# Two transformer blocks on one core: the first attention's causal mask moved from TensorE to VectorE, its subtraction to GpSimd, and a new order

## The reference

```python
def _mha(x, kv, Wq, Wk, Wv, mask, causal):          # 16 heads of 8
    energy = einsum('bhsk,bhtk->bhst', Q, K)
    lengths = sum(energy[:, :, 0, :] != 0, axis=-1)
    energy = where(cols >= lengths, -inf, energy)
    if causal:
        energy = where(cols[None, :] > cols[:, None], -inf, energy)
    score = softmax(energy / sqrt(dk))
    return einsum('bhst,bhtk->bhsk', score, V) * m

z  = _mha(x, x, Wq1, Wk1, Wv1, mask0, causal=True);         x1 = _layernorm(x + z)
z  = _mha(x1, context, Wq2, Wk2, Wv2, mask1, causal=False); x2 = _layernorm(x1 + z)
z  = (relu(x2 @ fc1_w.T + fc1_b) * mask0) @ fc2_w.T ...;    x3 = _layernorm(x2 + z)
scores = q_heads @ k_heads + bias + bias                    # second block, 16 heads of 64
out = _layernorm(softmax(scores) @ v_heads @ wo + bo + x3)
```

## Time and profile before

| | us |
|---|---|
| median of 3 runs | 342.96 |
| lowest, highest | 342.07, 342.99 |
| the profiled execution | 342.57 |
| its span, from the first to the last instruction | 340.8 |
| busy: TensorE, VectorE, GpSimd, ScalarE | 329.0, 290.3, 242.1, 240.8 |

### The profile page before, as it was taken

One profiled execution on the slowest core, in us unless ns is written; L12 is line 12 of the kernel. 1 busy time (PEld: TensorE's weight loads), 2 busy tenths in 40 slices (PEclk: granted clock), 3 DMA queues, 4 the chain that ended last, 5 costly groups with the idle time before them and its releaser, 6 DMA issues.

```text
span 340.8 us, 13283 instructions
## 1 busy us (share of the span) xinstructions
PE 329.0 (97%) x5363; PEld 255.6 (75%) x5363; DVE 290.3 (85%) x836; ACT 240.8 (71%) x567; POOL 242.1 (71%) x376
## 2 busy tenths in 40 slices
...
GB/s 153 339 305 223 2 2 2 2 4 4 125 2 64 3 12 2 63 80 56 11 4 72 10 63 4 80 4 2 2 2 136 4 70 2 3 20 125 17 2 25
DMA packets 13180, 17.88 MB, mean 52 GB/s; under 512 B 1600, under 2 KB 10176, under 8 KB 13120
## 3 DMA queue, kind: packets, MB, share of 16 engines
...
HBM read 15.99 MB, written 1.05 MB: 50 GB/s over the span
## 4 chain that ended last, share of the span: by engine, by line
PE 72%; DVE 12%; ACT 6%; issue 3%; POOL 3%; DMA 1%; SPq 1%; DVEq 0%; POOLq 0%
PE C_E L630 6%; PE C_E L575 6%; PE A_E L429 4%; PE C_E L620 4%; PE A_E L448 4%; PE C_E L591 4%; PE B_E L429 3%; PE B_E L448 3%; PE C_E L607 3%; PE B_E L346 3%; PE B_E L462 2%; PE A_E L462 2%; PE B_E L545 2%; PE B_E L547 2%; PE B_E L546 2%
## 5 line engine op out<-in xcount | busy, mean ns | idle before, releaser
L1019 POOL TENSOR_TENSOR A_kblk<-A_qk,cst 128x1024 f32<-128x1024 f32 x16 | 30.4, 1899 | 27.1 <-DVE A_qk L863 26.9
L1040 POOL TENSOR_TENSOR L_xg<-L_xh,vec_sb 128x128 f32<-128x128 f32 x64 | 30.2, 471 | 15.3 <-DVE L_xh L937 15.2
L1029 POOL TENSOR_TENSOR L_rstd<-L_ve,cst 128x1 f32<-128x1 f32 x64 | 35.2, 550 | 5.0
L1071 POOL TENSOR_TENSOR Sc<-Sc,C_mx 128x512 f32<-128x512 f32 x28 | 29.2, 1044 | 9.7 <-DVE C_mx L977 9.5
L761 ACT ACTIVATE qT<-C_E,bq 128x128 f32<-128x128 f32 x112 | 31.3, 380 | 4.0 <-PE C_E L575 3.8
L1027 POOL TENSOR_TENSOR L_ve<-L_mv,cst 128x1 f32<-128x1 f32 x64 | 12.3, 193 | 28.7 <-DVE L_mv L928 28.3
L1019 POOL TENSOR_TENSOR B_kblk<-B_qk,cst 128x1024 f32<-128x1024 f32 x16 | 30.4, 1899 | 0.5 <-DVE B_qk L863 0.3
L1080 POOL TENSOR_TENSOR Pc<-Pc,C_rd 128x512 f32<-128x512 f32 x28 | 29.0, 1044 | 1.2 <-DVE C_rd L987 1.0
L575 PE MATMUL C_E<-x3T,wq_sb 128*128 128x128 f32 x224 | 29.0, 277 | 0.4 <-ACT x3T L753 0.4
L575 PEld LDWEIGHTS C_E<-x3T,wq_sb 128*128 128x128 f32 x224 | 27.1, 192 | 1.1 <-ACT x3T L753 0.5
L630 PE MATMUL C_E<-wo_sb,C_zT 128*128 128x128 f32 x224 | 27.6, 276 | 0.1
...
## 6 DMA issues: line engine op xcount, KB each, us to landing
...
```

What stands on the lines that cost most here:

```text
L1019: tt(a.kblk[:], a.qk[:, 1].unsqueeze(1).to_broadcast([P, 8, P]), at["rmask"].unsqueeze(2).to_broadcast([P, 8, P]), ALU.mult).then_inc(a.s_ ...
L1029: tt(l.rstd[:], l.ve[:], at["power"], ALU.pow).then_inc(l.s_rstd, 1)
L1040: tt(l.xg[:], l.xh[:], l.g, ALU.mult).then_inc(l.s_xg, 1)
L1071: tt(v, v, place(n).mx[:, 8 * g:8 * g + 8].unsqueeze(2).to_broadcast([P, 8, S]), ALU.subtract).then_inc(C.s_sub, 1)
```

## The change

Chain A's mask leaves TensorE. The four products with eye64 and later are gone, and later becomes a tile of single-precision numbers. VectorE now adds it as it copies the energies out of PSUM (masked), and takes the maximum from the copy in SBUF (masked_max). The subtraction of the maximum is done in place by GpSimd (a_sub). Chain B keeps its way.

Beside this: the transpose of x3 goes to the second of C's banks, waits less, and leaves part of its waits to the projection behind it; the scaling of the last norm is a scalar_tensor_tensor with the reciprocal deviation as a broadcast tensor; of the 16 groups of fillers at the end 6 are left; and PLAN is another list.

```diff
+COOL = 6
-        eye64, later = sb("eye64", [P, S], BF16), sb("later", [P, S], BF16)
+        later = sb("later", [P, S])
...
             def warm_last(n):
+                if n >= COOL:
+                    return
                 pe.wait_ge(L2.s_xh, PAIRS)
                 idle_products(Bc.X[:, :], 3)
...
                             last = mm(bank[S * b:S * b + S, :], a.qk[r, 0, S * b:S * b + S],
-                                      a.kblk[r, :, S * b:S * b + S], start=True, stop=not causal,
-                                      skip_group_check=True)
-                    if causal:
-                        for hf, bank in enumerate((a.E, a.X)):
-                            r = slice(S * hf, S * hf + S)
-                            for b in range(2):
-                                last = mm(bank[S * b:S * b + S, :], eye64[r, :],
-                                          later[r, :].unsqueeze(1).to_broadcast([S, 8, S]),
-                                          start=False, stop=True, skip_group_check=True)
+                                      a.kblk[r, :, S * b:S * b + S], start=True, stop=True)
                     last.then_inc(a.s_e, 1)
...
                 elif n <= SPLIT:
                     pe.wait_ge(C.s_s, 2 * n)
-                    if n > 1:
-                        pe.wait_ge(L4.s_y, n - 1)
                 elif n == SPLIT + 1:
                     pe.wait_ge(L1.s_xh, PAIRS)
                 else:
-                    pe.wait_ge(L4.s_y, n - 1)
-                if n == 0:
-                    pe.wait_ge(bvo_ready, 2)
-                tr(place(n).E[0][:, 0:P], h2[n % RING][:], ident).then_inc(C.s_x3t, 1)
+                    pe.wait_ge(C.s_zts, 2 * n - 2)
+                tr(place(n).E[1][:, 0:P], h2[n % RING][:], ident).then_inc(C.s_x3t, 1)
...
                     if n == 0:
                         pe.wait_ge(w_queries, 16)
+                        pe.wait_ge(bvo_ready, 2)
+                    elif g == 0 and n > 1 and n != SPLIT + 1:
+                        pe.wait_ge(L4.s_y, n - 1)
...
-                act.copy(place(n).x3T[:], place(n).E[0][:, 0:P]).then_inc(C.s_x3ts, 1)
+                act.copy(place(n).x3T[:], place(n).E[1][:, 0:P]).then_inc(C.s_x3ts, 1)
...
+            def masked(hf):
+
+                def step(n):
+                    dve.wait_ge(A.s_e, n + 1)
+                    if n:
+                        dve.wait_ge(A.s_pt, 2 * n - 1 + hf)
+                    if hf == 0 and n == 0:
+                        dve.wait_ge(ready, 2)
+                    tt(heads(A.S[:, hf * HALF:(hf + 1) * HALF]), heads((A.E, A.X)[hf][:, :]),
+                       later[:].unsqueeze(1).to_broadcast([P, 8, S]), ALU.add).then_inc(A.s_msk, 1)
+                return step
+
+            def masked_max(hf):
+
+                def step(n):
+                    dve.wait_ge(A.s_msk, 2 * n + 1 + hf)
+                    dve.tensor_reduce(A.mx[:, 8 * hf:8 * hf + 8], heads(A.S[:, hf * HALF:(hf + 1) * HALF]), AX.X, ALU.max
+                                      ).then_inc(A.s_max, 1)
+                return step
...
-                    ts(l.xh[:], l.y, l.mv[:, 0:1], l.rstd[:, 0:1], ALU.subtract, ALU.mult).then_inc(l.s_xh, 1)
+                    if l is L4:
+                        dve.scalar_tensor_tensor(l.xh[:], l.y, l.mv[:, 0:1], l.rstd[:].to_broadcast([P, D]),
+                                                 ALU.subtract, ALU.mult).then_inc(l.s_xh, 1)
+                    else:
+                        ts(l.xh[:], l.y, l.mv[:, 0:1], l.rstd[:, 0:1], ALU.subtract, ALU.mult).then_inc(l.s_xh, 1)
...
+            def a_sub(hf):
+
+                def step(n):
+                    pool.wait_ge(A.s_max, 2 * n + 1 + hf)
+                    v = heads(A.S[:, hf * HALF:(hf + 1) * HALF])
+                    tt(v, v, A.mx[:, 8 * hf:8 * hf + 8].unsqueeze(2).to_broadcast([P, 8, S]),
+                       ALU.subtract).then_inc(A.s_sub, 1)
+                return step
...
 PLAN = """
-A.qkv#0 A.qk#0 A.q0#0 A.e0#0 A.nz#0 A.cnt#0 K.warm#0 C.chi#0 A.cut#0 C.whi#0 A.v#0 K.warm#1 A.kblk#0 C.wlo#0
+K.warm#0 A.qkv#0 A.qk#0 A.q0#0 A.e0#0 A.nz#0 C.chi#0 A.cnt#0 K.warm#1 A.cut#0 C.whi#0 A.v#0 K.warm#2 A.kblk#0
...
```

More of the change, by code:

```diff
@@ L412, in cnt, with energy @@
                 return step
[L414 removed]
+            def energy(a, l):
                 def step(n):
@@ L634, in _ @@
             steps = {"K.warm": warm_first, "L.warm": warm_last, "B.tr": b_tr, "B.f1": f1, "B.f2": f2, "B.f3": f3, "C.x3t": c_x3t, "C.e": c_e, "C.zt": c_zt, "C.o": c_o, "C.bvo": bvo,
-                     "A.qkv": qkv(A, [W[n] for n in ("Wq1", "Wk1")]), "A.e": energy(A, L1, True),
-                     "B.qkv": qkv(Bc, [W[n] for n in ("Wq2", "Wk2")]), "B.e": energy(Bc, L2, False)}
+                     "A.qkv": qkv(A, [W[n] for n in ("Wq1", "Wk1")]), "A.e": energy(A, L1),
+                     "B.qkv": qkv(Bc, [W[n] for n in ("Wq2", "Wk2")]), "B.e": energy(Bc, L2)}
             for g in range(2):
@@ L802, in _ @@
             dve.tensor_copy(ofb[:], at["bsel"]).then_inc(ready, 1)
-            ts(later[:], iota[:], at["trow"], BIG, ALU.is_gt, ALU.mult)
-            ts(eye64[:], iota[:], at["trow"], None, ALU.is_equal).then_inc(ready, 1)
+            ts(later[:], iota[:], at["trow"], BIG, ALU.is_gt, ALU.mult).then_inc(ready, 1)
             def wlo(n):
@@ L1002, in _ @@
             for nm, a in (("A", A), ("B", Bc)):
-                steps |= {nm + ".q0": q0(a), nm + ".v": v(a), nm + ".nz": nz(a), nm + ".cut": cutk(a), nm + ".zn": zn(a),
-                          nm + ".max_0": maximum(a, 0), nm + ".max_1": maximum(a, 1),
-                          nm + ".sub_0": sub(a, 0), nm + ".sub_1": sub(a, 1)}
+                steps |= {nm + ".q0": q0(a), nm + ".v": v(a), nm + ".nz": nz(a), nm + ".cut": cutk(a), nm + ".zn": zn(a)}
             for g in range(2):
+                steps |= {f"A.msk_{g}": masked(g), f"A.max_{g}": masked_max(g),
+                          f"B.max_{g}": maximum(Bc, g), f"B.sub_{g}": sub(Bc, g)}
                 steps |= {f"C.fadd_{g}": fadd(g), f"C.max_{g}": c_max(g), f"C.den_{g}": den(g)}
@@ new lines @@
+C.ks_0#1 A.pv_1#0 A.zts#0 C.ks_1#1 A.z#0 C.k_0#2 A.zn#0 C.k_1#2 A.y#0 C.ks_0#2 A.st#0 C.ks_1#2 C.k_0#3
+A.rstd#0 C.chi#4 C.k_1#3 A.xh#0 C.ks_0#3 C.wvlo#0 A.gb#0 A.e#1 C.ks_1#3 C.clo#4 B.am#0 C.v_0#0 A.msk_0#1
+B.cm#0 A.qk#2 C.v_1#0 C.vs_0#0 A.max_0#1 B.tr#0 A.msk_1#1 C.k_0#4 A.sub_0#1 B.xts#0 A.q0#2 A.max_1#1 B.qkv#0
+A.exp_0#1 A.e0#2 A.sub_1#1 C.vs_1#0 A.pt_0#1 A.nz#2 B.qk#0 C.k_1#4 A.exp_1#1 B.q0#0 A.pts_0#1 A.pt_1#1
+A.pv_0#1 A.pts_1#1 A.cnt#2 C.ks_0#4 A.cut#2 A.pv_1#1 B.e0#0 A.v#2 A.zts#1 A.kblk#2 C.ks_1#4 A.z#1 B.nz#0
@@ new lines @@
+C.pts_0#1 A.msk_0#6 C.pt_1#1 C.st#0 B.kblk#4 C.v_1#4 A.max_0#6 C.pts_1#1 C.vs_0#4 A.msk_1#6 C.zt#1 C.vs_1#4
+A.q0#7 B.am#5 B.gb#3 B.v#4 B.e#4 C.zts_0#1 A.max_1#6 B.cm#5 A.sub_0#6 C.zts_1#1 B.f1#3 B.max_0#4 A.e0#7
+B.f1s#3 B.max_1#4 A.sub_1#6 B.f2#3 A.exp_0#6 C.e#2 B.sub_0#4 B.f2s#3 C.x3c#1 B.sub_1#4 A.exp_1#6 C.rstd#0
+B.f3#3 B.exp_0#4 C.fadd_0#2 A.pt_0#6 B.exp_1#4 B.y3#3 B.pt_0#4 A.pts_0#6 A.pt_1#6 A.nz#7 B.3st#3 B.pts_0#4
+B.pt_1#4 C.max_0#2 A.pts_1#6 B.3rstd#3 B.pv_0#4 A.pv_0#6 C.fadd_1#2 B.pts_1#4 A.pv_1#6 C.sub_0#2 A.cnt#7
@@ new lines @@
+C.exp_1#9 B.y#11 B.st#11 C.qs_1#10 C.k_0#14 C.den_1#9 B.rstd#11 C.k_1#14 C.ks_0#14 A.v#14 C.pt_0#9 C.nrm_1#9
+B.nz#12 C.ks_1#14 B.xh#11 A.qkv#15 C.pts_0#9 B.cnt#12 A.e#14 B.gb#11 B.cut#12 B.v#12 A.gb#13 C.pt_1#9
+A.msk_0#14 B.f1#11 C.v_0#12 A.msk_1#14 B.f1s#11 B.kblk#12 A.qk#15 C.pts_1#9 B.f2#11 A.max_0#14 C.v_1#12
+B.f2s#11 A.max_1#14 C.vs_0#12 B.f3#11 C.vs_1#12 C.zt#9 C.st#8 A.sub_0#14 B.y3#11 B.e#12 B.3st#11 A.sub_1#14
+A.exp_0#14 A.q0#15 B.am#13 C.zts_0#9 A.e0#15 B.max_0#12 B.3rstd#11 A.exp_1#14 A.pt_0#14 B.max_1#12 C.zts_1#9
```

304 lines of the change are left out of this document (146 added, 158 removed).

## The result

The changed kernel takes 346.9 us (median of four runs, 345.07 to 347.65) where the kernel before takes 342.65 in the same batch (342.07 to 342.99). The ratio is 1.0118, with a 95% interval from 1.0098 to 1.0138, so 3.4 to 4.7 us more. The prediction had said 339.6 us, 335.3 to 344.2: wrong in sign, and outside its range.

The account below looks back on a forecast made before the run. The prediction took the sum of TensorE's work to bound most of the span: 342.57 - 3.5 (mask) + 1.0 (start) - 0.5 (tail) = 339.6 us, all else at 0; range for 8 in 10: 335.3 to 344.2.

Parts of the forecast that it names:

- 16 x 0.22 = 3.5 us less: Mask products leaving TensorE: 16 groups of four, each priced at its 0.22 us in the chain of waits, 3.5 us less.
- Rival 2: VectorE, not TensorE, is the bound; the mask's 3.5 us turn into waits: 343.1 us, chance 0.18 together with the cold tail.
- The start: First pairs: fillers moved earlier and the longer way in pairs 0 and 1 cost +1.0 us, bounds 0 and +2.4.
- The fillers: Start: two more before the first energies, which come later by 2 x 0.43 us; 0.54 us of fillers at 36.99 go.
- the mask's longer way: From energies to first transposes: 1.0 us more way; of 2.0 us in pairs 0 and 1, 0.6 was taken.
- The tail: End of the kernel: the transpose of x3 and its copy run beside the earlier pair's sum, 0.5 us less.
- The form of L_xh: Last norm's scaling with the scale as a broadcast tensor: at most 3 us of VectorE's time, off the path; taken as 0.
- GpSimd's 33.4 us at nothing on the path: GpSimd takes 32 subtractions, busy 242.1 to 275.5 us; taken at nothing on the path, bounds 0 and 10 us.
- the sign that the prediction had set: Wrong if the first attention's transposes wait for the exponential by more than 0.2 us a pair.
- the cover that hides it: TensorE's work before the first transposes: 0.9 us more in the new lists, against 1.0 us more way.
- Rival 3: GpSimd becomes the limiter, subtractions queue behind blocks of keys and norms, TensorE stands: 344.8 us, chance 0.15.

Follow-up runs that it names:

- E13: The kernel before with the mask's four TensorE products a pair left out and nothing in their place: 342.58 us, ratio 1.0001.
- E17: The kernel before with VectorE made lighter, one cross attention sum (C.den_0) taken over 16 of 64 columns a head: 342.11 us, ratio 0.9975.
- E8: The kernel before with only the new order's start, up to A.e#3, taken over: 344.55 us, ratio 1.0061.
- E15: The kernel before with only the start's six groups of fillers moved to where the new order has them: 342.26 us, ratio 1.0000.
- E1: The changed kernel with VectorE's A.m0#4 (maximum over four pairs and a 128x4 comparison) moved back right behind B.am#2: 345.32 us, ratio 1.0069.
- E2: The kernel before with A.m0#4 alone moved late, behind A.cut#4, as GpSimd begins a block of keys: 346.05 us, ratio 1.0081.
- E12: The kernel before, order and mask unchanged, with x3's transpose to the other bank, the last norm's new form and 6 end filler groups: 342.58 us, ratio 1.0006.
- E5: The changed kernel with the last norm's L_xh as a tensor_scalar again: 346.52 us, ratio 1.0121.
- E3: The kernel before, in its old order, with the mask edit alone (VectorE adds the mask, GpSimd subtracts): 367.43 us, ratio 1.0697.
- E4: The changed kernel's new order and small edits, with the mask on TensorE and the subtraction on VectorE as before: 354.65 us, ratio 1.0339.
- E16: The kernel of E1 with the start's six groups of fillers back where the kernel before has them: 344.00 us, ratio 1.0052.

## Why the prediction was wrong

**The step that failed is "16 x 0.22 = 3.5 us less".** It rested on the chain of waits: the mask's products stood in it as pieces of their own, TensorE was busy 275.38 of 280 us, "so what is taken from that list comes off the time, as long as nobody makes TensorE wait instead". E13 takes exactly that away and measures 0.0 us (-0.2 to +0.3). The condition at the end of that sentence decided. A piece in the chain says who released the next step last, not by how much: with the mask gone TensorE stands and waits instead, in many places by half a microsecond and less, and its busy share of 98% hid that it was so near to waiting. Rival 2 had given the mask this price, nothing, but its reason fits only half: E17 shows that VectorE alone doesn't set the pace either. Of the rule of the Trainium skill that the prediction weighed (Perfetto Trace Analysis, Identifying the Most-Contended Engine), the warning on matmuls' busy share held, with 3.2 us less of it for 0.0 us. That the engine with the highest occupancy, VectorE, is then the one to relieve first brought little here, 0.9 us for 5.5.

**The start, "+1.0, bounds 0 and +2.4"**, was mis-sized: 2.1 (1.5 to 2.7) by E8, and for another reason. The fillers, 0.86 of the term, cost nothing in the old order (E15), and the mask's longer way is not in E8 at all; the order of the other steps is what is left.

**A.m0#4 was not in the sum at all.** The prediction followed steps that the change edits, and took the new order as neutral behind the start. Of the moved steps this one landed beside a GpSimd instruction of 1.90 us: 1.7 us by E1, 2.8 by E2. With the start it makes up the loss, by these prices; the failed term explains only why nothing was gained.

**The tail, "-0.5"**: 0 (E12, with the other small edits), and from B.e#15 to the end 0.2 us more. **The form of L_xh**, taken at 0: 0 (E5). The rule of the Trainium skill that the prediction cited (SBUF — State Buffer, Who interferes with whom), of two SBUF inputs, agrees with the 1.15 us beside a GpSimd subtraction of 1.04; the form with one tile waits as well, 1.09 us at the same place.

**GpSimd's 33.4 us at nothing on the path**: the busy time was right (274.0 for 275.5), and as far as the profile shows the price too. From B.e#2 to B.e#15 the balance is 0.3 us, and the sign that the prediction had set, transposes that wait for the exponential, is not there. But the cover that hides it is the new order's work, and in the old order the same edit costs 24 us (E3). Rival 3's queue is met there; in the changed kernel the chain goes through it once, from 252.74 to 257.32 us. That rival 3's 344.8 came nearest is no merit of its reason.

Laid together from 342.65: 0 for the mask, 2.1 for the start, 1.7 to 2.8 for A.m0#4 with its clock, 0 for the rest: 346.5 to 347.6, where 346.9 was measured. These prices come from different kernels, and E3 and E4 show that parts don't add everywhere, so the agreement is no proof. Open are which steps of the start cost the 2.1 us, what makes up E16's last 1.8 us over the kernel before, and which waits exactly took the mask's place in E13: the longest that are new have 0.5 us. So what sets the pace of the kernel before in place of TensorE's work is not shown. No kernel that computes the whole result beat the kernel before.
